# A fused attention and expert block on one core: the query side reads turned rows back from device memory, its steps move one place earlier, and the residual's bias is one operation

## The chip, the cores and the metric

One core of a Trainium2 chip. The metric is device time in microseconds (us), lower is better. Shapes: x is 8 x 2048 rows of 256 floats; everything is float32 (some matmuls take operands split into a high and a low part).

## The reference, cut to what matters

```
q, k, v = heads(x @ Wq + bq), heads(x @ Wk + bk), heads(x @ Wv + bv)      # 16 heads of 16
qp = relu(q @ rw) + 1e-6 ;  kp = relu(k @ rw) + 1e-6                       # 64 features a head
kv = sum over a sequence of kp' v
out = (qp @ kv) / (qp . sum(kp) + 1e-6) ;  x1 = layernorm(x + out @ Wo + bo)
prob = 4 heads' top-8 experts of 1024, from x1 @ Wrq @ keys (exp, products of two halves, keep, normalise)
y = (silu(x1 @ Wg + bg) * (x1 @ Wu + bu)) @ Wd + bd  +  (silu(x1 @ down') * prob) @ up
x2 = layernorm(x1 + y)
```

## The kernel before

The rows are cut into 32 groups of 512; four groups make a sequence. After a start that takes the key side of groups 0 to 3, the program is a loop of **rounds** (`body`, called by `schedule`), numbered from 4 to 38. In round `it` five stages run side by side, each on its own group: the key side ("kv") on group it, the query side of attention ("at") on group m = it - 4, the choice of experts ("rt") on it - 5, the two feed-forward products ("ff") on it - 6, and the last layernorm on it - 7. So rounds 7 to 31 hold all stages. In rounds 8, 12, ..., 32 a finished sequence is folded into attention's weights as well ("fold", "consts").

A round has 8 **slots**, c = 0 to 7, one for each 128 columns of the feed-forward. In a slot PE runs a fixed frame: gate(c), up(c), [choice of experts rt(c/2) where c is even], dots(c), transposes pt(c), and the output matmuls of slot c - 1 in two halves. The frame has three **places**, early, mid and late, where one step of the query side can stand (`AT_EARLY`, `AT_MID`, `AT_LATE`: every third entry of `AT_SEQ`), and likewise places for the key side's steps (`KV_SEQ`). The order in each engine's program is thus written out; an engine runs it strictly in that order.

Steps of the query side: turn0, turn1 (transposes of the group's rows `xb`, 4 matmuls each; ACT copies them to `xbT`, which is `qp[:, 2:4]`), q0, q1 (projection; ACT writes the high parts, DVE the low parts), qp0 to qp7 (features; ACT applies relu), den0 + num0 and den1 + num1 (4 + 4 matmuls with attention's weights), divide0, divide1 (on DVE), wo0, wo1, and at the end of the round next0, next1 (transposes of x1). The key side has turn, k, v, kp0 to kp7 and sum; ACT reads each kp out of PSUM.

All steps but gate, up, dots and the outputs share four PSUM banks, `step_bank`. A **planner** (`take`, line by line through the whole program) gives each use the bank that by its tables `WORK` and `HOLD` comes free first; the table entry for kp is `"kp": 2.0`. At run time PE waits before each use until the reader of the use before it in that bank is done:

```
def free(eng, *use):
    k, nth = place[use]
    if nth:
        eng.wait_ge(bank_read[k], nth)
```

Readers: DVE reads rt(t) in `scores(t)` (L1123), ACT reads kp at L856. In slot 2 and 4 ACT runs, in this order, exp(t) of the scores (`rt_use`, L892, with a table load before and after), then the late kp, then the next slot's silu of gate (L917). In odd slots `mask` (L906, L911) waits for that silu, then POOL's products `spread` (L479) and DVE's `keep` and `add_head` (L1147, L1157, L1160) follow, and then the next slot's scores. In each odd slot DVE's add_head of head 2 runs beside a product of POOL.

POOL adds attention's bias to `xb` (L466, after turn1), and the feed-forward's bias to the residual, which a DMA brings into `prob` columns that pt(0) to pt(3) have freed (L509, slot 5, two operations). SP's queue, in this order: next key rows (L400), output rows (L403), residual (L407), next query rows `xb` and the copy of x1 (L411, L412).

Of the kernel before, what the change touches and what calls it, by code (L numbers as in the profile page):

```python
# [27 lines left out]
P = 128  # L28


def block_kernel(nc, x, Wq, bq, Wk, bk, Wv, bv, Wo, bo, rw, Wg, bg, Wu, bu, Wd, bd,
# [29 lines left out]
              + [("v", 1)] + KV_TILE[2] + KV_TILE[3])  # L61
    AT_SEQ = ([[("turn", 0)], [("turn", 1)], [("q", 0)], [("q", 1)]] + [[("qp", j)] for j in range(4)] + [[]]
              + [[("den", 0), ("num", 0)], [("divide", 0), ("qp", 4)]] + [[("qp", j)] for j in range(5, 8)] + [[]]
              + [[("den", 1), ("num", 1)], [("divide", 1)], [], [("wo", 0)], [("wo", 1)], []])
    KV_USES = len(KV_SEQ)
# [5 lines left out]
    with ExitStack() as ctx:  # L71
# [56 lines left out]
        gate = sb("gate", P, 2, G)  # L128
        wexp = sb("wexp", P, 2, G)
        y_sb = x1  # L130
        x1_kept = nc.dram_tensor("x1_kept", [NG, P, T, D], F32).ap()
# [28 lines left out]

        xa2_loaded = sem("xa2_loaded")
        k2_high = sem("k2_high")

# [133 lines left out]
        class Lane:  # L297


            def __init__(self, x, xT, k_hl, kp, v, xs, loaded, high):  # L300
                self.x, self.xT, self.k_hl, self.kp, self.v, self.xs = x, xT, k_hl, kp, v, xs
                self.loaded, self.high = loaded, high

        xs_total = xs[:, 2]
        LANES = [Lane(xa, xaT, kT_hl, kp, v_sb, xs[:, 0], xa_loaded, k_high),
                 Lane(xb, xbT, qT_hl, kp2, v2_sb, xs[:, 1], xa2_loaded, k2_high)]
        main, second = LANES

# [53 lines left out]
        def _(sp):  # L362
# [33 lines left out]
            def body(it, par, kv, at, rt, ff, last, batch):
                a, m, n, f = it, it - ATTN_LAG, it - FFN_LAG, it - LAST_LAG
                if a + 1 < NG:
                    sp.wait_ge(*full("kv", a, "turn", 1))
                    sp.dma_start(xa[:], x_groups[a + 1]).then_inc(xa_loaded, 16)  # L400
                if last:
                    sp.wait_ge(y_ready, (f + 1) * T)
                    sp.dma_start(out_groups[f], y_sb[:]).then_inc(y_stored, 16)  # L403
                if ff:
                    sp.wait_ge(*full("pt", n, C // 2 - 1))
                    sp.wait_ge(x1_stored, (n + 1) * 16)
                    sp.dma_start(residual(par), x1_kept[n].rearrange("p (i t) d -> p i (t d)", i=2)).then_inc(res_loaded, 16)  # L407
# [11 lines left out]
        def _(pool):  # L419
# [39 lines left out]
            def body(it, par, kv, at, rt, ff, last, batch):  # L459
                a, m, s, n, f = it, it - ATTN_LAG, it - ROUTE_LAG, it - FFN_LAG, it - LAST_LAG  # L460
                if at:
                    pool.wait_ge(xb_loaded, (m + 1) * 16)
                    pool.wait_ge(*full("at", m, "turn", 1))
                    if m == 0:
                        pool.wait_ge(bo_ready, 2)
                    pool.tensor_tensor(xb[:], xb[:], bcast(bo_sb[:].unsqueeze(1), [P, T, D]),  # L466
                                       ALU.add).then_inc(xb_bias, 1)
# [20 lines left out]
                for c in range(C):  # L488
                    t, odd = divmod(c, 2)
                    kv_adds(KV_FIRST[c])  # L490
                    if rt and odd:
                        spread(t, 2)
                    if last and c == 0:
                        norm_scale(y_dve, (f + 1) * Y_STEPS, ln2_pool, f, mv2, rstd2, rstd2_ready)
                    kv_adds(KV_EARLY[c])
                    if rt and odd:
                        spread(t, 3)
                    if at and c == 6:
                        norm_scale(at_dve, (m + 1) * AT_STEPS, ln1_pool, m, mv1, rstd1, rstd1_ready)
                    if rt and not odd:  # L500
                        spread(t, 0)
                    kv_adds(KV_LATE[c])
                    if rt and not odd:
                        spread(t, 1)
                    if ff and c == 5:
                        pool.wait_ge(res_loaded, (n + 1) * 16)
                        rows = residual(par).rearrange("p i (t d) -> p i t d", t=2)
                        for i in range(2):
                            pool.tensor_tensor(rows[:, i], rows[:, i], bcast(bd_sb[:].unsqueeze(1), [P, 2, D]),  # L509
                                               ALU.add).then_inc(res_bias, 1)  # L510

# [4 lines left out]
        def _(pe):  # L516
# [144 lines left out]
            def body(it, par, kv, at, rt, ff, last, batch):  # L661
# [14 lines left out]
                def at_use(kind, j):  # L676
# [3 lines left out]
                    free(pe, "at", m, kind, j)  # L680
                    if kind == "turn":
                        if j == 0:
                            pe.wait_ge(xb_loaded, (m + 1) * 16)
                        mm = turn(at_bank, xb, j)
                    elif kind == "q":
                        pe.wait_ge(*drained("at", m, "turn", 1))
                        mm = project(at_bank, wq_sb, xbT, j)
# [121 lines left out]
        def _(act):  # L809
# [31 lines left out]
            def kv_use(a, kind, j):  # L841
# [5 lines left out]
                if kind == "turn":  # L847
                    if j == 0 and i:
                        before = a - 1 if a > 2 * FILL else a - 2
                        act.wait_ge(xs_added, before + before // BG + 1)  # L850
                    read_by(act.activation(lane.xT[:, j, :], bank[:], ACT.Identity,
                                           accum_out=lane.xs[:, j:j + 1]), "kv", a, kind, j)
# [10 lines left out]
            def body(it, par, kv, at, rt, ff, last, batch):  # L863
# [3 lines left out]
                def at_use(kind, j):  # L867
# [3 lines left out]
                    act.wait_ge(*full("at", m, kind, j))  # L871
                    if kind == "turn":
                        read_by(act.copy(xbT[:, j, :], at_bank[:]), "at", m, kind, j)
                    elif kind == "q":
                        highs(qT_hl, j, at_bank, bq_sb, q_high)
# [84 lines left out]
        def _(dve):  # L960
# [102 lines left out]
            def body(it, par, kv, at, rt, ff, last, batch):  # L1063
# [121 lines left out]
                def y_rows():  # L1185
# [6 lines left out]
                    dve.wait_ge(x1_stored, (min(m, NG)) * 16)  # L1192
                    dve.wait_ge(res_bias, (f + 1) * 2)
                    rows = residual(other).rearrange("p i (t d) -> p i t d", t=2)
# [88 lines left out]
```

## Time and profile before

| | |
|---|---|
| runs shown | 3479.89, 3481.85, 3484.04 us |
| median | 3481.85 us |
| profiled execution, its own time | 3480.97 us |
| its span, first to last instruction | 3479.1 us |
| granted clock of TensorE, mean | 0.989 |

PE is TensorE's matmuls, PEld its weight loads, DVE VectorE, ACT ScalarE, POOL GpSimd, SP SyncE. In a timeline a row reads: start us, busy us, engine, line, operation, written<-read, count, and in brackets the idle time before it with what ended it. Matmuls overlap, so a step's price on PE is best read from the start of one row to the start of the next. Line numbers are those of the kernel before.

### The profile page before, as it was taken

How to read it: one execution, taken by the hardware profiler on the slowest of the kernel's cores; microseconds unless marked ns; L12 is line 12 of the kernel's file. 1: busy time of each engine (PE TensorE's matmuls, PEld its weight loads, DVE VectorE, ACT ScalarE, POOL GpSimd, SP SyncE). 2: the span in 40 equal slices, each digit the busy share in tenths (PEclk: the TensorE clock that was granted, in tenths of full speed). 3: DMA queues.
4: the chain of work that ended last, by engine and by line, in shares of the span. 5: the costliest groups of instructions: out<-in, count | busy, mean ns of one | idle time of the engine just before them, and what ended most of it. 6: DMA issues, size and time to landing. Idle time of an engine off the chain costs nothing.

```text
span 3479.1 us, 48605 instructions
## 1 busy us (share of the span) xinstructions
PE 3362.4 (97%) x17888; PEld 2641.6 (76%) x17888; DVE 2870.6 (83%) x5316; ACT 1991.4 (57%) x2886; POOL 1301.9 (37%) x788
## 2 busy tenths in 40 slices
PE   8779999999999999999999999999999999999988
PEld 6457877777777777877777877777877777777767
DVE  4688878988888888888888887888888888888873
ACT  4456556555556555566556566556556565555541
POOL 0234333334333434343334343344333344434441
PEclk9889999999999999999999999999999999999999
DMA  4000000100001000000001000100000000000000
GB/s 122 25 19 31 19 19 31 31 25 31 19 19 31 31 25 31 19 19 31 31 25 31 19 19 31 31 25 31 19 19 31 31 19 25 25 19 25 13 19 19
DMA packets 36762, 94.35 MB, mean 27 GB/s; under 512 B 6832, under 2 KB 11184, under 8 KB 36528
## 3 DMA queue, kind: packets, MB, share of 16 engines
q1 hardware_dynamic: 36528, 91.25, 8.2%
q8 instruction: 145, 2.38, 0.3%
q14 instruction: 89, 0.73, 0.1%
HBM read 57.68 MB, written 33.55 MB: 26 GB/s over the span
## 4 chain that ended last, share of the span: by engine, by line
PE 82%; DVE 7%; ACT 6%; issue 3%; POOL 2%; DMA 0%; SPq 0%; POOLq 0%; ACTq 0%; DVEq 0%
PE ring L672 26%; PE y_bank L757 11%; PE y_bank L759 11%; PE step_bank L574 6%; PE step_bank L566 5%; PE step_bank L672 4%; PE step_bank L610 3%; PE step_bank L602 3%; PE step_bank L701 3%; PE step_bank L691 3%; PE step_bank L745 3%; DVE prob L1160 2%; PE step_bank L560 2%; POOL grid L479 1%; ACT prob L911 1%
## 5 line engine op out<-in xcount | busy, mean ns | idle before, releaser
L479 POOL TENSOR_TENSOR grid<-ex 128x1024 f32<-128x1024 f32 x512 | 994.5, 1950 | 1469.6 <-ACT ex L892 726.5
L757 PE MATMUL y_bank<-wd_sb,gate 128*128 128x256 f32 x2048 | 622.8, 386 | 9.2 <-DVE wexp L1182 9.2
L759 PE MATMUL y_bank<-up_sb,wexp 128*128 128x256 f32 x2048 | 613.3, 381 | 0.0
L1160 DVE SCALAR_TENSOR_TENSOR prob<-grid,narrow,prob 128x1024 f32<-128x1024 f32 x256 | 580.2, 2266 | 9.0
L672 PE MATMUL ring<-x1T_hl,downT_hl 128*128 128x512 f32 x1536 | 421.2, 410 | 23.8 <-ACT gate L917 23.7
L672 PE MATMUL ring<-x1T_hl,wg_hl 128*128 128x512 f32 x1536 | 430.1, 415 | 5.0 <-DVE gate L1176 5.0
L759 PEld LDWEIGHTS y_bank<-up_sb,wexp 128*128 128x128 f32 x2048 | 391.8, 191 | 54.2
L1147 DVE SCALAR_TENSOR_TENSOR grid<-grid,best 128x1024 f32<-128x1024 f32 x256 | 343.6, 1342 | 107.0 <-POOL grid L479 105.1
L672 PE MATMUL ring<-x1T_hl,wu_hl 128*128 128x512 f32 x1536 | 421.2, 409 | 0.0
L757 PEld LDWEIGHTS y_bank<-wd_sb,gate 128*128 128x128 f32 x2048 | 362.0, 192 | 70.8 <-issue 37.9
L672 PEld LDWEIGHTS ring<-x1T_hl,wu_hl 128*128 128x128 f32 x1536 | 281.9, 188 | 119.6 <-issue 42.9
L672 PEld LDWEIGHTS ring<-x1T_hl,downT_hl 128*128 128x128 f32 x1536 | 277.4, 189 | 97.3 <-ACT gate L917 36.8
L672 PEld LDWEIGHTS ring<-x1T_hl,wg_hl 128*128 128x128 f32 x1536 | 286.1, 189 | 75.8 <-issue 14.9
L856 ACT ACTIVATE kp<-step_bank 128x512 f32<-128x512 f32 x233 | 137.3, 590 | 339.4 <-PE step_bank L602 339.3
L1176 DVE SCALAR_TENSOR_TENSOR gate<-ring,bu_sb,gate 128x512 f32<-128x512 f32 x256 | 190.5, 744 | 165.6 <-PE ring L672 157.9
L892 ACT ACT_TABLE_LOAD x124 | 159.1, 1283 | 284.0 <-DVE ex L1125 283.4
L922 ACT ACTIVATE wexp<-ring 128x512 f32<-128x512 f32 x256 | 152.3, 595 | 283.0 <-PE ring L672 282.2
L917 ACT ACTIVATE gate<-ring,bg_sb 128x512 f32<-128x512 f32 x256 | 176.3, 689 | 237.8 <-PE ring L672 235.4
L906 ACT ACTIVATE grid<-grid,narrow 128x1024 f32<-128x1024 f32 x256 | 294.1, 1149 | 11.4 <-POOL grid L479 6.8
L1086 DVE RECIPROCAL x<-x 128x512 f32<-128x512 f32 x64 | 213.9, 3343 | 2.6 <-ACT x L884 2.6
L672 PE MATMUL step_bank<-route_hl,x1T_hl 128*128 128x512 f32 x768 | 198.6, 394 | 1.8 <-DVE x1T_hl L970 1.8
L466 POOL TENSOR_TENSOR xb<-xb,bo_sb 128x1024 f32<-128x1024 f32 x32 | 75.5, 2358 | 303.7 <-PE step_bank L560 303.7
(168 smaller groups left out, 5551.2 us busy)
## 6 DMA issues: line engine op xcount, KB each, us to landing
xb<-in_L_attn_x SPq DMA_DIRECT2D x34, 512.0 KB, 4.2
x_kept<-x SPq DMA_DIRECT2D x32, 512.0 KB, 5.1
prob<-x_kept SPq DMA_DIRECT2D x32, 512.0 KB, 3.6
out_y<-x SPq DMA_DIRECT2D x32, 512.0 KB, 2.7
xa<-in_L_attn_x SPq DMA_DIRECT2D x30, 512.0 KB, 3.5
prob<-in_L_ffn_down_embed SPq DMA_DIRECT2D x1, 1024.0 KB, 6.2
prob<-in_L_ffn_Wg SPq DMA_DIRECT2D x1, 1024.0 KB, 10.0
prob<-in_L_ffn_Wu SPq DMA_DIRECT2D x1, 1024.0 KB, 10.7
```

What stands on the lines that cost most here:

```text
L479: pool.tensor_tensor(grid[:, h % 2], bcast(ex[:, h, 0:NX].unsqueeze(2), [P, NX, NK]), bcast(ex[:, RH + h, 0:NK].unsqueeze(1), [P, NX, NK]) ...
L566: mm = pe.matmul(bank[:], w[:, k, e * P:(e + 1) * P], srcT[:, k, :], start=(k == 0), stop=(k == KD - 1))
L574: mm = pe.matmul(bank[:, (t - t0) * D:(t - t0 + 1) * D], srcT[:, k, t * P:(t + 1) * P], w[:, k, :], start=(k == 0), stop=(k == KD - 1))
L672: mm = pe.matmul(bank[:], st if swap else wt, wt if swap else st, start=(k == 0 and i == 0), stop=(k == KD - 1 and i == 2))
L757: pe.matmul(rows, gate[:, c % 2, t * P:(t + 1) * P], wd_sb[:, c, :], start=(c == 0 and t % 2 == 0), stop=False, skip_group_check=True)
L759: mm = pe.matmul(rows, wexp[:, c % 2, t * P:(t + 1) * P], up_sb[:, c, :], start=False, stop=(c == C - 1), skip_group_check=True)
L906: act.activation(g, g, ACT.Prelu, bias=drop[:, h:h + 1], alpha=STEEP).then_inc(bent, 1)
L917: act.activation(gate[:, c % 2], ring[c % 2][:], ACT.Silu, bias=bg_sb[:, c:c + 1]).then_inc(ring_act, 1)
L1086: at_steps.mark(dve.reciprocal(rows, rows))
L1147: marks["keep", h] = rt_steps.mark(dve.scalar_tensor_tensor(out=g, in0=g, scalar=best[:, h, TOP - 1:TOP], in1=g, op0=ALU.is_ge, op1=ALU.mult))
L1160: ins = dve.scalar_tensor_tensor(out=row, in0=g, scalar=rz[:, h:h + 1], in1=row, op0=ALU.mult, op1=ALU.add, accum_out=mass[:, 0:1] if h == ...
L1176: dve.scalar_tensor_tensor(out=gate[:, c % 2], in0=ring[1 - c % 2][:], scalar=bu_sb[:, c:c + 1], in1=gate[:, c % 2], op0=ALU.add, op1=ALU. ...
```

## The change

Three edits. (1) After a group's key side has turned its rows (`xT`), SP stores them to device memory (`xT_kept`, one DMA of 512 KB a group); in the round before their query side they are loaded into `xbT` once num1 has been issued and read its operands. turn0 and turn1 of the query side, their ACT copies, and PE's wait for `xb` are gone; POOL's bias on `xb` no longer waits for turn1. (2) `AT_SEQ` loses its two turn entries and gets one empty entry ahead and one behind: q1 stands late in slot 0 instead of early in slot 1, qp to wo1 one place earlier, den0 and num0 late in slot 2 instead of early in slot 3, den1 and num1 late in slot 4 instead of early in slot 5. divide0 and divide1 on DVE now stand ahead of slot 3's and slot 5's product with up(c). The planner runs anew over the new order, with its tables as they were. (3) The residual's bias is one POOL operation in slot 4, ahead of the first product of that slot, instead of two at the end of slot 5.

```diff
-    AT_SEQ = ([[("turn", 0)], [("turn", 1)], [("q", 0)], [("q", 1)]] + [[("qp", j)] for j in range(4)] + [[]]
+    AT_SEQ = ([[], [("q", 0)], [("q", 1)]] + [[("qp", j)] for j in range(4)] + [[]]
               + [[("den", 0), ("num", 0)], [("divide", 0), ("qp", 4)]] + [[("qp", j)] for j in range(5, 8)] + [[]]
-              + [[("den", 1), ("num", 1)], [("divide", 1)], [], [("wo", 0)], [("wo", 1)], []])
+              + [[("den", 1), ("num", 1)], [("divide", 1)], [], [("wo", 0)], [("wo", 1)], [], []])
...
+        xT_kept = nc.dram_tensor("xT_kept", [NG, P, KD, G], F32).ap()
...
+            def keep_turned(a):
+                sp.wait_ge(*drained("kv", a, "turn", 0))
+                sp.wait_ge(*drained("kv", a, "turn", 1))
+                sp.dma_start(xT_kept[a], in_lane(a)[0].xT[:]).then_inc(in_lane(a)[0].kept, 16)
...
                     sp.dma_start(xa[:], x_groups[a + 1]).then_inc(xa_loaded, 16)
+                if kv:
+                    keep_turned(a)
...
+                if at and m + 1 < NG:
+                    lane, i = in_lane(m + 1)
+                    sp.wait_ge(*full("at", m, "num", 1))
+                    sp.wait_ge(lane.kept, (i + 1) * 16)
+                    sp.dma_start(xbT, xT_kept[m + 1]).then_inc(xbT_loaded, 16)
                 if at:
                     sp.wait_ge(x1_ready, (m + 1) * T)
...
                     pool.wait_ge(xb_loaded, (m + 1) * 16)
-                    pool.wait_ge(*full("at", m, "turn", 1))
...
+                    if ff and c == C // 2:
+                        pool.wait_ge(res_loaded, (n + 1) * 16)
+                        rows = residual(par).rearrange("p i (t d) -> p i t d", t=2)
+                        pool.tensor_tensor(rows, rows, bcast(bd_sb[:].unsqueeze(1).unsqueeze(1), [P, 2, 2, D]),
+                                           ALU.add).then_inc(res_bias, 1)
                     if rt and not odd:
                         spread(t, 0)
...
-                    if ff and c == 5:
-                        pool.wait_ge(res_loaded, (n + 1) * 16)
-                        rows = residual(par).rearrange("p i (t d) -> p i t d", t=2)
-                        for i in range(2):
-                            pool.tensor_tensor(rows[:, i], rows[:, i], bcast(bd_sb[:].unsqueeze(1), [P, 2, D]),
-                                               ALU.add).then_inc(res_bias, 1)
...
-                    if kind == "turn":
-                        if j == 0:
-                            pe.wait_ge(xb_loaded, (m + 1) * 16)
-                        mm = turn(at_bank, xb, j)
-                    elif kind == "q":
-                        pe.wait_ge(*drained("at", m, "turn", 1))
+                    if kind == "q":
+                        pe.wait_ge(xbT_loaded, (m + 1) * 16)
                         mm = project(at_bank, wq_sb, xbT, j)
...
+                        act.wait_ge(lane.kept, i * 16)
...
-                    if kind == "turn":
-                        read_by(act.copy(xbT[:, j, :], at_bank[:]), "at", m, kind, j)
...
-                    dve.wait_ge(res_bias, (f + 1) * 2)
+                    dve.wait_ge(res_bias, f + 1)
```

**PE, slot 0, from rt(0) to gate(1) of round 15, before** (route_hl is rt(0), ident_r,xa the key side's turn, ident_r,xb the query side's, downT_hl dots(0), ident_r,prob pt(0), qp,wq_sb the projection q; bank_readN counts the readers of step_bank N):

```order
L672 MATMUL step_bank<-route_hl,x1T_hl 128x512 [waits bank_read2,bank_read1,bank_read3]
L672 MATMUL ring<-x1T_hl,downT_hl 128x512 [waits ring_act]
L560 MATMUL step_bank<-ident_r,xb 128x128 [waits bank_read1]
L745 MATMUL step_bank<-ident_r,prob 128x128 [waits bank_read0,prob_ready]
L560 MATMUL step_bank<-ident_r,xa 128x128 [waits bank_read3]
L566 MATMUL step_bank<-qp,wq_sb 128x512 [waits bank_read1]
L672 MATMUL ring<-x1T_hl,wg_hl 128x512 [waits h_ready]
L566 MATMUL step_bank<-qp,wq_sb 128x512 [waits bank_read1,bank_read3]
```

**The same place after:**

```order
L692 MATMUL step_bank<-route_hl,x1T_hl 128x512 [waits bank_read0,bank_read3,bank_read2]
L692 MATMUL ring<-x1T_hl,downT_hl 128x512 [waits ring_act]
L586 MATMUL step_bank<-qp,wq_sb 128x512 [waits xbT_loaded,bank_read2]
L761 MATMUL step_bank<-ident_r,prob 128x128 [waits bank_read3,prob_ready]
L580 MATMUL step_bank<-ident_r,xa 128x128 [waits bank_read1]
L586 MATMUL step_bank<-qp,wq_sb 128x512 [waits xbT_loaded,bank_read0]
L692 MATMUL ring<-x1T_hl,wg_hl 128x512 [waits h_ready]
```

q1 stands ahead of gate(1), and the planner has given it bank 0, which in this round rt(0) filled: q1 waits for the read of rt(0). Before, q1 had the bank of the key side's turn1. So it is in rounds 7 to 31 but for those with a fold, where q1 has q0's bank.

**PE, end of slot 2 and start of slot 3, before** (rw_hl,kT_hl is kp, L701 with four waits den0, with one wait num0; the outputs between are left out):

```order
L745 MATMUL step_bank<-ident_r,prob 128x128 [waits bank_read3]
L602 MATMUL step_bank<-rw_hl,kT_hl 128x256 [waits bank_read3,bank_read1]
L672 MATMUL ring<-x1T_hl,wg_hl 128x512 [waits h_ready]
L701 MATMUL step_bank<-qp,kv_blocks 32x512 [waits bank_read1,bank_read3,blocks_ready,bank_read0]
L701 MATMUL step_bank<-qp,kv_blocks 32x512 [waits bank_read2]
L672 MATMUL ring<-x1T_hl,wu_hl 128x512 [waits ring_act]
```

**The same place after:**

```order
L761 MATMUL step_bank<-ident_r,prob 128x128 [waits bank_read0]
L622 MATMUL step_bank<-rw_hl,kT_hl 128x256 [waits bank_read2]
L717 MATMUL step_bank<-qp,kv_blocks 32x512 [waits bank_read2,bank_read3,blocks_ready,bank_read0]
L717 MATMUL step_bank<-qp,kv_blocks 32x512 [waits bank_read2]
L692 MATMUL ring<-x1T_hl,wg_hl 128x512 [waits h_ready]
```

den0 and num0 stand ahead of gate(3), and num0 has the bank that kp0 filled just before it, in all of rounds 6 to 31; before, num0 had the bank of rt(1). In the same way num1 has the bank of kp3: there it had it before too, but num1 now stands ahead of gate(5).

**ACT, slot 2 into slot 3, after** (ex is exp(1), kp the read of kp0, x<-step_bank the read of den0, gate the silu of gate(3)):

```order
L907 ACT_TABLE_LOAD [waits rt_dve]
L907 ACTIVATE ex<-ex 128x576 [waits bank_read1]
L873 ACTIVATE kp<-step_bank 128x512 [waits bank_full3]
L899 ACTIVATE x<-step_bank,consts 128x512 [waits x1_stored,bank_read3,y_stored,bank_full2]
L932 ACT_TABLE_LOAD [waits y_full]
L932 ACTIVATE gate<-ring,bg_sb 128x512 [waits ring_full]
```

The read of kp0 still stands behind exp(1), which waits for DVE's scores(1); the read of den0 has come in ahead of the silu of gate(3).

## Rows read from the trace of the kernel before

**Rows 1.** The page: busy time, share of the span and instructions of each engine.
```profile
PE 3362.4 (97%) x17888; PEld 2641.6 (76%) x17888; DVE 2870.6 (83%) x5316; ACT 1991.4 (57%) x2886; POOL 1301.9 (37%) x788
```

**Rows 2.** Stretches: us, busy by engine, clock, DMA share, GB/s; rounds 15, 16, 33.
```profile
1159.58:1262.38 102.80, 102.80 (x547) 80.94 (x545) 89.24 (x165) 62.19 (x90) 40.90 (x25) 1.00 0.09 26
1262.38:1370.60 108.22, 106.45 (x599) 83.66 (x597) 89.23 (x172) 62.42 (x90) 40.62 (x24) 1.00 0.07 25
3027.30:3122.90 95.60, 89.09 (x419) 69.91 (x417) 82.55 (x155) 53.28 (x74) 40.76 (x23) 0.98 0.07 23
```

**Rows 3.** Timeline of PE, round 15, slots 0 and 1.
```profile
1166.16 0.60 PE L560 MATMUL step_bank<-ident_r,xb 128*128 128x128 f32 x4
1166.60 0.60 PE L745 MATMUL step_bank<-ident_r,prob 128*128 128x128 f32 x4
...
1167.58 1.95 PE L566 MATMUL step_bank<-qp,wq_sb 128*128 128x512 f32 x4
1168.97 1.95 PE L672 MATMUL ring<-x1T_hl,wg_hl 128*128 128x512 f32 x6
```

**Rows 4.** Timeline of PE, round 15: gate(3), den0 with num0, gate(5).
```profile
1195.84 1.73 PE L672 MATMUL ring<-x1T_hl,wg_hl 128*128 128x512 f32 x6
1197.50 1.92 PE L701 MATMUL step_bank<-qp,kv_blocks 128*32 128x512 f32 x16
...
1219.79 1.72 PE L672 MATMUL ring<-x1T_hl,wg_hl 128*128 128x512 f32 x6
```

**Rows 5.** Timeline of DVE, round 15: scores(0), scores(1), keep and add beside POOL's bias.
```profile
1169.23 0.69 DVE L1123 TENSOR_TENSOR ex<-step_bank,top 128x512 f32<-128x512 f32 x1
...
1195.49 0.69 DVE L1123 TENSOR_TENSOR ex<-step_bank,top 128x512 f32<-128x512 f32 x1
...
1214.28 1.28 DVE L1160 SCALAR_TENSOR_TENSOR prob<-grid,narrow,prob 128x1024 f32<-128x1024 f32 x1
...
1237.26 1.71 DVE L1147 SCALAR_TENSOR_TENSOR grid<-grid,best 128x1024 f32<-128x1024 f32 x1
1239.01 2.20 DVE L1160 SCALAR_TENSOR_TENSOR prob<-grid,narrow,prob 128x1024 f32<-128x1024 f32 x1
```

**Rows 6.** Timeline of ACT, round 15: q0's highs, silu(1), mask(0), exp(1), kp0, silu(3), kp3.
```profile
1169.57 1.39 ACT L838 ACTIVATE qT_hl<-step_bank,bq_sb 64x512 fp32r<-64x512 f32 x2 [1.21 <-PE step_bank L566]
...
1174.28 0.69 ACT L917 ACTIVATE gate<-ring,bg_sb 128x512 f32<-128x512 f32 x1
...
1176.72 0.48 ACT L901 ACTIVATE narrow<-best,narrow 128x1 f32<-128x1 f32 x2 [0.23 <-DVE narrow L1141]
1177.23 1.15 ACT L906 ACTIVATE grid<-grid,narrow 128x1024 f32<-128x1024 f32 x1
...
1196.39 1.28 ACT L892 ACT_TABLE_LOAD   x1 [3.91 <-DVE ex L1125]
...
1198.27 0.58 ACT L856 ACTIVATE kp<-step_bank 128x512 f32<-128x512 f32 x1
...
1200.17 0.69 ACT L917 ACTIVATE gate<-ring,bg_sb 128x512 f32<-128x512 f32 x1
...
1220.50 0.58 ACT L856 ACTIVATE kp<-step_bank 128x512 f32<-128x512 f32 x1
```

**Rows 7.** Timeline of POOL, round 15: attention's bias, the residual's bias.
```profile
1166.91 2.37 POOL L466 TENSOR_TENSOR xb<-xb,bo_sb 128x1024 f32<-128x1024 f32 x1 [8.44 <-PE step_bank L560]
...
1235.62 4.51 POOL L509 TENSOR_TENSOR prob<-prob,bd_sb 128x512 f32<-128x512 f32 x2
```

**Rows 8.** The page, DMA issues: count, KB each, us from issue to landing.
```profile
x_kept<-x SPq DMA_DIRECT2D x32, 512.0 KB, 5.1
```

**Rows 9.** Waits of PE in its timeline (rounds 16, 33).
```profile
1287.75 1.98 PE L566 MATMUL step_bank<-xaT,wk_sb 128*128 128x512 f32 x4 [1.71 <-ACT qp L877]
...
3117.86 1.02 PE L757 MATMUL y_bank<-wd_sb,gate 128*128 128x256 f32 x2 [2.30 <-DVE wexp L1182]
```

**Rows 10.** Stretch behind the second of those waits, columns as in rows 2.
```profile
3117.86:3121.23 3.37, 3.37 (x8) 2.66 (x9) 3.33 (x2) 0.00 (x0) 1.90 (x1) 0.53 0.30 118
```

More of the change, by code:

```diff
@@ L161, in block_kernel @@
         xa2_loaded = sem("xa2_loaded")
+        xaT_kept, xbT_kept, xbT_loaded = sem("xaT_kept"), sem("xbT_kept"), sem("xbT_loaded")
         k2_high = sem("k2_high")
@@ L297, in block_kernel, with __init__ @@
         class Lane:
-            def __init__(self, x, xT, k_hl, kp, v, xs, loaded, high):
+            def __init__(self, x, xT, k_hl, kp, v, xs, loaded, kept, high):
                 self.x, self.xT, self.k_hl, self.kp, self.v, self.xs = x, xT, k_hl, kp, v, xs
-                self.loaded, self.high = loaded, high
+                self.loaded, self.kept, self.high = loaded, kept, high
         xs_total = xs[:, 2]
-        LANES = [Lane(xa, xaT, kT_hl, kp, v_sb, xs[:, 0], xa_loaded, k_high),
-                 Lane(xb, xbT, qT_hl, kp2, v2_sb, xs[:, 1], xa2_loaded, k2_high)]
+        LANES = [Lane(xa, xaT, kT_hl, kp, v_sb, xs[:, 0], xa_loaded, xaT_kept, k_high),
+                 Lane(xb, xbT, qT_hl, kp2, v2_sb, xs[:, 1], xa2_loaded, xbT_kept, k2_high)]
         main, second = LANES
@@ L389, in _ @@
                     sp.dma_start(lane.x[:], x_groups[2 * r + k]).then_inc(lane.loaded, 16)
+                for k in range(2):
+                    keep_turned(2 * (r - 1) + k)
             sp.wait_ge(*full("kv", 2 * FILL - 2, "turn", 1))
@@ L394, in _ @@
             sp.dma_start(xb[:], x_groups[0]).then_inc(xb_loaded, 16)
+            for k in range(2):
+                keep_turned(2 * FILL - 2 + k)
+            sp.wait_ge(*full("kv", 2 * FILL - 1, "v", 1))
+            sp.wait_ge(xbT_kept, FILL * 16)
+            sp.wait_ge(xaT_kept, 16)
+            sp.dma_start(xbT, xT_kept[0]).then_inc(xbT_loaded, 16)
             def body(it, par, kv, at, rt, ff, last, batch):
@@ L871, in at_use @@
                     act.wait_ge(*full("at", m, kind, j))
-                    if kind == "turn":
-                        read_by(act.copy(xbT[:, j, :], at_bank[:]), "at", m, kind, j)
-                    elif kind == "q":
+                    if kind == "q":
                         highs(qT_hl, j, at_bank, bq_sb, q_high)
```

## Prediction

> **What bounds the kernel now.** First the page's busy times: PE is busy in 97% of the span, DVE in 83%, POOL in 37% [rows 1]. That is an average, so next the stretches by round, from gate(0) to gate(0). In round 15 PE is busy in all of 102.80 us: it never waits, and its order is a sum of work. The fold's round 16 takes 108.22 with 1.8 of waits; in the tail's round 33 PE is busy for 89.09 of 95.60, so there others set the pace [rows 2]. Rounds 7 to 31 are of the first two kinds, 19 without and 6 with a fold. There a matmul taken from PE is time gained, but only as long as PE still finds at each place what it waits for. So I read PE's rows for the places of the change, and then when the reader of each step bank is done.
>
> **What PE loses in work.** From a turn's start to that of the next step are 0.44 us [rows 3], two turns 0.87. Over 25 rounds that is 22 us. ACT's two copies go too; ACT is busy for 62 of 102.80 us [rows 2], and they count only where ACT's order is on the path (below).
>
> **What moves: three waits.** All times are in round 15's frame, gate(0) at 1159.58.
>
> *q1.* It now precedes gate(1), at PE's 1168.97 - 0.87 = 1168.10 [rows 3], in the bank of rt(0). DVE reads that last in scores(0), until 1169.23 + 0.69 = 1169.92 [rows 5]. So PE, which had no wait, stands for 1.8. POOL's bias on `xb` (2.37, [rows 7]) no longer waits for turn1, and falls beside DVE's keep and add of the end of the round before. The nearest row of such company is keep beside POOL's other bias, 1.71 against 1.28 [rows 5]. I add that 0.4 (bounds 0 and 0.9, what add loses there): q1 starts at 1170.3, a wait of 2.2. On ACT, q1's high parts now precede exp(0). High parts start 2.0 after their matmul (1169.57 against 1167.58, [rows 3, 6]), so at 1172.3, 2.7 later than those of q0 that stood there. exp(0), silu(1) and mask(0) follow. From silu(1) to mask(0) were 2.95, in which q1's high parts (1.39) go and a qp's read comes (priced as kp's, 0.58), and 0.23 was idle [rows 6]. So mask(0) is later by 2.7 - 1.39 + 0.58 - 0.23 = 1.65, and I take the chain behind it (POOL's product, DVE's keep, add and scores(1), ACT's exp(1)) as late by as much. Bounds: 0, if slack swallows it, and 2.7.
>
> *num0.* It now precedes gate(3), right behind kp0 and in kp0's bank. ACT's read of kp0 stands behind exp(1), whose table load waited 3.91 us for DVE's scores(1); it ended at 1198.27 + 0.58 = 1198.85 [rows 5, 6]. den0 with num0 take 1197.50 to 1199.35, the 1.85 between two neighbours, num0 half of it. PE alone would come to num0 at 1195.84 - 0.87 + 0.92 = 1195.9 [rows 3, 4], 2.95 ahead of the read even if nothing else moved. With the 1.65 the read ends at 1200.5: PE has lost 4.6 by then, q1's wait within it. Gate(3) follows at 1201.4, where the same work stood at 1195.84 + 1.85 = 1197.69: **+3.75** a round, the turns' gain included.
>
> *num1.* It now precedes gate(5), in kp3's bank. PE comes to it 23.95 - 0.92 = 23.0 after gate(3) [rows 4], at 1224.4. The read of kp3 ended at 1220.50 + 0.58 = 1221.08, behind exp(2), which hangs on slot 3's chain from silu(3). That began at 1200.17 [rows 6]; now it follows gate(3) (its matmuls take 1.66, [rows 4]) and begins about 1203.0: 2.8 later. Then the residual's bias: one operation at the end of slot 3's products, where it meets keep and add of head 3. In slot 5 those took 1.71 and 2.20 instead of 1.28 each, 1.35 in all [rows 5]; I take that (bounds: 0 if they don't meet, 1.9 if the add of head 2 meets it as well). The read then ends at 1221.08 + 4.15 = 1225.2, 0.8 behind PE: **+0.8** (0 to 1.4). DVE's time in slot 5 gets shorter by the same 1.35, but PE doesn't wait there.
>
> **Other rounds.** The sum of a round is 4.55. In fold rounds the fold's matmuls stand ahead of q1, which takes q0's bank, so part of the wait is covered; between -0.87 and +4.55 I take +1, that is +6 in all. Round 6 has num0 in kp0's bank too, but fewer stages: +2. The tail's four rounds have no kp and shed the turns and DVE's collisions: -1 each.
>
> **What I cost at nothing.** The store of turned rows and their load are 512 KB each, with 5.1 us to land [rows 8]; the DMA engines are busy for 0.09 of a round [rows 2]. The store goes out at about 1169, ahead of the output's store on SP, which waits longer for its rows. The load goes out once num1 has read its operands, over 40 us ahead of the next q0. If it were late, q0 would wait by as much. It stands ahead of x1's copy on SP, and is gone long before. divide0 and divide1 move ahead of the product with up(c) on DVE; that product's reader is a slot away. One bias operation in place of two: between 2.37, POOL's row of the same size, and 4.51 [rows 7]; POOL is busy for 40.90 of 102.80, and the next product waits for exp(2).
>
> **Sum.** 19 x 4.55 + 6 + 2 - 4 = +90.5 us on the profiled execution's 3480.97: 3571.5. The median of the runs is 0.9 above that execution, so I forecast **3572 us**.
>
> On the collisions: the trace has POOL's bias of 4.51 cost DVE 1.35, under a third of it [rows 5, 7]. The Trainium skill (SBUF — State Buffer, "SBUF: two separate sides") calls the port pair that VectorE and GpSimd share an exclusive lock: whoever starts first keeps it for its whole instruction, and the other fully blocks. By that, keep, starting some 0.6 into a bias of 2.37, would lose about 1.75 instead of 1.35, an estimate that adds 0.4 x 19 = 8 us. The sum goes by the row.
>
> **Rivals.** (1) *Only PE's work goes.* If kp0's read comes 2.95 or more earlier against gate(0), no bank wait holds. The point that decides is DVE's scores(1). For it: DVE idles for 13.5 us of the round [rows 2], so its order could close up. Against it: mask(0) now hangs on q1's high parts, later and not earlier. Gain 25 x 0.87 = 22: 3460, **faster**. Chance 0.11. (2) *Gain and wait cancel*, or the new places are neutral because kp0's read comes about 2 us sooner: 3482. Chance 0.05. (3) *Only num0 waits*; q1 delays nothing behind it, num1 finds its bank: 2.95 - 0.87 = 2.1 a round, 19 x 2.1 - 4 = +36, **3517**. For it: slack that a chain swallows is easily overlooked. Against: the 0.23 of idle on ACT is little [rows 6]. Chance 0.18. (4) *The forecast*: 0.54. (5) *The clock falls as well.* After a wait of 2.30 in round 33 TensorE ran at a granted 0.53 (its 1.2 GHz level) for 3.37 us, at a cost of 3.37 x 0.47 = 1.6; after one of 1.71 it stayed at 2.4 GHz [rows 9, 10]. The new waits, 2.2 and 2.4, are of that size. After q1 the loss would be hidden in num0's wait; after num0 it counts: 19 x 1.6 = 30, **3602**. Chance 0.12. The Trainium skill (TensorE: Matmul & The Clock Gate, "What's actually happening") has the throttled clock as the default that activity releases, which speaks for (5); the row of 1.71 shows that not every pause brings it back.
>
> **How the numbers follow.** My own case with its bounds reaches from 3540 (chain late by less) to 3600 (2.7 late). Down to 3510 the range takes in rival 3, up to 3612 rival 5 with a little more; outside are rivals 1 and 2 and small rests. A measurement of this kernel tells about 0.2%, 7 us, from no change. Faster is rival 1, 0.11; same is rival 2, 0.05; slower is all the rest, 0.84.
>
> **What would show it.** In the profile after: PE busy for less than a round; rounds such as 15 at about 107 us; waits of PE ahead of q1 of about 2 with DVE's scores as releaser, ahead of num0 of about 2.4 on ACT's read of kp, ahead of num1 under 1.4; the turns on `xb` gone; POOL's residual bias as one row of 2.4 to 4.5, with keep and add of slot 3 longer and those of slot 5 at 1.28; mask(0) about 19.3 us behind gate(0) instead of 17.65. I am wrong if rounds take about 102, if kp0's read ends within 36.3 us of gate(0), or if q0 waits for its load.

## The result, and the profile after

The changed kernel takes **3588.42 us** (median of 4 runs, 3586.83 to 3593.29), beside 3480.87 for the kernel before on the same chip: a ratio of 1.0312, 95% interval 1.0298 to 1.0327. That is slower by 107.5 us; 3572 were forecast, with 3510 to 3612 as the range.

The page after, busy times and the chain that ended last, against [rows 1]:

```profile
PE 3373.8 (94%) x17632; PEld 2617.2 (73%) x17632; DVE 2851.4 (79%) x5316; ACT 1956.9 (55%) x2822; POOL 1312.5 (37%) x756
...
PE 35%; DVE 28%; ACT 19%; issue 13%; POOL 4%; SPq 0%; ACTq 0%; DVEq 0%; DMA 0%; POOLq 0%
```

PE has 256 matmuls fewer, the turns, and is busy for 11 us more than before (3362.4). Where the time came from is read by rounds. These are sums of rounds of the profiled execution (3589.75 us), each from gate(0) to gate(0) in the timeline of PE, in us, with the change in the last column:

| stretch | before | after | change | forecast |
|---|---|---|---|---|
| ahead of round 6 | 219.9 | 219.6 | -0.3 | 0 |
| round 6 | 104.8 | 107.4 | +2.6 | +2 |
| 19 rounds without a fold, of 7 to 31 | 1953.4 | 2043.9 | +90.5 | +86.5 |
| their median round | 102.79 | 107.23 | +4.44 | +4.55 |
| 6 rounds with a fold | 650.9 | 663.5 | +12.6 | +6 |
| rounds 32 to 36 | 472.0 | 475.2 | +3.2 | -4 |

Stretches after (rounds 14, 15, 16 and 34; columns as in [rows 2]):

```profile
1085.03:1192.26 107.23, 102.66 (x538) 79.79 (x537) 88.04 (x165) 61.11 (x88) 41.06 (x24) 1.00 0.10 35
1192.26:1300.89 108.63, 104.30 (x539) 80.46 (x537) 88.23 (x165) 61.11 (x88) 41.31 (x25) 0.98 0.10 35
1300.89:1411.58 110.69, 107.73 (x590) 83.20 (x589) 89.75 (x172) 61.22 (x88) 41.02 (x24) 0.98 0.10 34
3228.32:3324.61 96.29, 88.91 (x410) 68.75 (x409) 83.15 (x155) 52.30 (x72) 40.34 (x23) 0.98 0.08 28
```

Round 14 is the typical one: PE is busy for 102.66, where round 15 before had 102.80 without a gap, and idle for 4.57. Its idle time stands in PE's timeline: q0 and pt(0) (no wait), then q1, gate(1), dots(1), den0, num0, gate(3), num1.

```profile
1091.15 1.88 PE L586 MATMUL step_bank<-qp,wq_sb 128*128 128x512 f32 x4
1092.87 0.60 PE L761 MATMUL step_bank<-ident_r,prob 128*128 128x128 f32 x4
...
1095.80 1.98 PE L586 MATMUL step_bank<-qp,wq_sb 128*128 128x512 f32 x4 [1.90 <-DVE ex L1138]
1097.22 1.94 PE L692 MATMUL ring<-x1T_hl,wg_hl 128*128 128x512 f32 x6
...
1103.27 1.65 PE L692 MATMUL ring<-x1T_hl,downT_hl 128*128 128x512 f32 x6 [0.56 <-ACT gate L932]
...
1123.79 1.06 PE L717 MATMUL step_bank<-qp,kv_blocks 128*32 128x512 f32 x8 [0.28 <-DVE v_sb L1031]
1125.72 1.07 PE L717 MATMUL step_bank<-qp,kv_blocks 128*32 128x512 f32 x8 [0.87 <-ACT kp L873]
1126.72 1.66 PE L692 MATMUL ring<-x1T_hl,wg_hl 128*128 128x512 f32 x6
...
1150.83 1.07 PE L717 MATMUL step_bank<-qp,kv_blocks 128*32 128x512 f32 x8 [0.96 <-ACT kp L873]
```

The three bank waits are there, each with the releaser that was named: DVE's scores (L1138), ACT's read of kp (L873) twice. ACT in that round, mask(0), kp0, silu(3), kp3:

```profile
1104.19 1.15 ACT L921 ACTIVATE grid<-grid,narrow 128x1024 f32<-128x1024 f32 x1
...
1125.09 0.58 ACT L873 ACTIVATE kp<-step_bank 128x512 f32<-128x512 f32 x1
...
1128.42 0.69 ACT L932 ACTIVATE gate<-ring,bg_sb 128x512 f32<-128x512 f32 x1 [0.86 <-PE ring L692]
...
1150.20 0.58 ACT L873 ACTIVATE kp<-step_bank 128x512 f32<-128x512 f32 x1
```

mask(0) starts 1104.19 - 1085.03 = 19.16 after gate(0); it was 17.65, and 19.3 was forecast. DVE in the same round (keep at its start; in slot 3 the add of head 2, then keep and add of head 3), then POOL (bias on `xb`, last product of slot 3, the residual's bias):

```profile
1086.71 1.65 DVE L1162 SCALAR_TENSOR_TENSOR grid<-grid,best 128x1024 f32<-128x1024 f32 x1
...
1137.58 3.03 DVE L1175 SCALAR_TENSOR_TENSOR prob<-grid,narrow,prob 128x1024 f32<-128x1024 f32 x1
...
1141.13 2.81 DVE L1162 SCALAR_TENSOR_TENSOR grid<-grid,best 128x1024 f32<-128x1024 f32 x1
1143.97 1.28 DVE L1175 SCALAR_TENSOR_TENSOR prob<-grid,narrow,prob 128x1024 f32<-128x1024 f32 x1
```

```profile
1083.87 3.41 POOL L487 TENSOR_TENSOR xb<-xb,bo_sb 128x1024 f32<-128x1024 f32 x1
...
1137.62 1.91 POOL L500 TENSOR_TENSOR grid<-ex 128x1024 f32<-128x1024 f32 x1 [3.13 <-DVE prob L1172]
1139.49 3.37 POOL L524 TENSOR_TENSOR prob<-prob,bd_sb 128x1024 f32<-128x1024 f32 x1
```

Both biases now meet a keep, which takes 1.65 and 2.81, where a DVE operation of this size takes 1.28 alone [rows 5], and POOL's own operation takes 3.4 instead of the 2.37 of [rows 7]: it begins while DVE's add is still running.

### The profile page after: what moved, and what is told of

It is laid out like the page before. It is cut to its first block, busy times and chain, and to the rows that moved or that the text cites. A ratio compares the mean times of both kernels' runs of the same rounds, so it can differ in the third digit from the quotient of the medians.

```text
span 3587.9 us, 48061 instructions
## 1 busy us (share of the span) xinstructions
PE 3373.8 (94%) x17632; PEld 2617.2 (73%) x17632; DVE 2851.4 (79%) x5316; ACT 1956.9 (55%) x2822; POOL 1312.5 (37%) x756
## 4 chain that ended last, share of the span: by engine, by line
PE 35%; DVE 28%; ACT 19%; issue 13%; POOL 4%; SPq 0%; ACTq 0%; DVEq 0%; DMA 0%; POOLq 0%
PE ring L692 10%; DVE prob L1175 7%; DVE grid L1162 5%; PE step_bank L594 5%; POOL grid L500 4%; PE y_bank L773 4%; ACT grid L921 4%; PE y_bank L775 4%; ACT prob L926 3%; DVE prob L1172 3%; PE step_bank L586 3%; DVE top L1135 3%; ACT L932 2%; PE step_bank L630 2%; PE step_bank L717 2%
## 5 line engine op out<-in xcount | busy, mean ns | idle before, releaser
L500 POOL TENSOR_TENSOR grid<-ex 128x1024 f32<-128x1024 f32 x512 | 1011.2, 1982 | 1540.3 <-ACT ex L907 794.7
L1162 DVE SCALAR_TENSOR_TENSOR grid<-grid,best 128x1024 f32<-128x1024 f32 x256 | 391.0, 1527 | 284.9 <-POOL grid L500 283.1
L1175 DVE SCALAR_TENSOR_TENSOR prob<-grid,narrow,prob 128x1024 f32<-128x1024 f32 x256 | 551.5, 2154 | 7.9
L692 PE MATMUL ring<-x1T_hl,wu_hl 128*128 128x512 f32 x1536 | 399.7, 396 | 0.0
L873 ACT ACTIVATE kp<-step_bank 128x512 f32<-128x512 f32 x233 | 136.9, 589 | 416.1 <-PE step_bank L622 416.0
L692 PEld LDWEIGHTS ring<-x1T_hl,wu_hl 128*128 128x128 f32 x1536 | 289.9, 189 | 64.0
L477 POOL TENSOR_SCALAR rstd<-mv 128x4 f32<-128x4 f32 x64 | 15.2, 237 | 602.7 <-DVE mv L1091 602.7
```

The source lines that it names most:

```text
L500: pool.tensor_tensor(grid[:, h % 2], bcast(ex[:, h, 0:NX].unsqueeze(2), [P, NX, NK]), bcast(ex[:, RH + h, 0:NK].unsqueeze(1), [P, NX, NK]) ...
L692: mm = pe.matmul(bank[:], st if swap else wt, wt if swap else st, start=(k == 0 and i == 0), stop=(k == KD - 1 and i == 2))
L1162: marks["keep", h] = rt_steps.mark(dve.scalar_tensor_tensor(out=g, in0=g, scalar=best[:, h, TOP - 1:TOP], in1=g, op0=ALU.is_ge, op1=ALU.mult))
L1175: ins = dve.scalar_tensor_tensor(out=row, in0=g, scalar=rz[:, h:h + 1], in1=row, op0=ALU.mult, op1=ALU.add, accum_out=mass[:, 0:1] if h == ...
```

## The experiments

Each ran against the kernel before on the same chip; before's median was 3479 to 3483 us in all of them. Behind each time stand its ratio to that and the 95% interval of the ratio. "Steady" is the median round without a fold in the profiled execution.

**Places back, the rest as changed.**

```diff
-    AT_SEQ = ([[], [("q", 0)], [("q", 1)]] + ...
+    AT_SEQ = ([[], [], [("q", 0)], [("q", 1)]] + ...
```

> Turned rows from device memory and the one bias as in the changed kernel, but the query side's steps at the places of the kernel before (the two turn entries left empty). Bank theory (the loss is PE waiting at the new places for banks that DVE and ACT still hold): no wait is left, PE saves the turns, 25 x 0.87 less some dearer neighbours: 3455 to 3470 us, rounds of 102.0 to 102.4. Rival, the bias theory (the residual's bias beside slot 3's keep and add makes the chain late): slower than before, 3490 to 3520.

Measured: 3494.65 us, 1.0036 (1.0023 to 1.0048), steady 103.49. So 94 of the 107 us hang on the new places; but the turns' time isn't gained, and 12 us are lost: at the old places the time is in the bias theory's range. Waits of PE's weight loads in one round (total, times, longest, in us), and POOL and DVE in slot 3 (view by view):

```profile
PEld step_bank L717 <- ACT kp L873: 1.1, 1, 1.1
...
PEld ring L692 <- DVE gate L1191: 0.9, 1, 0.9
```

```profile
1106.42 3.38 POOL L524 TENSOR_TENSOR prob<-prob,bd_sb 128x1024 f32<-128x1024 f32 x1
```

```profile
1108.07 2.81 DVE L1162 SCALAR_TENSOR_TENSOR grid<-grid,best 128x1024 f32<-128x1024 f32 x1
```

With the turns gone PE comes to gate(1) sooner, and its weight load waits for DVE's product with up(0); PE's own rows show a gap of only 0.10 there (q0 from 1061.30 to 1063.18, gate(1) at 1063.28), although q0's start and gate(1)'s lie 1.98 apart instead of 1.39 [rows 3]: the rows of two steps overlap, and a wait takes that overlap first. And keep loses 1.53; in slot 5 num1's weight load then waits 1.1 for ACT's read of kp.

**Other banks for num0 and num1; for q1; for all three** (one number each in the planner's table; both are shown, as the third run has them).

```diff
-        ... "kp": 2.0, ... "rt": 8.0
+        ... "kp": 6.0, ... "rt": 12.0
```

> The changed kernel, but the planner's table holds a kp's bank for 6 instead of 2: num0 then has the bank of rt(1), num1 that of pt(4), q1 still that of rt(0). Bank theory: the waits of 0.87 ahead of num0 and 0.96 ahead of num1 go in 25 rounds (the second alone in fold rounds): 3588 - 19 x 1.83 - 6 x 0.96 = 3548; rounds of 105.4. Rival, the chain theory (ACT and DVE are themselves late, because q1's high parts stand ahead of exp(0)): PE stops a little later for a silu or for weights instead, 3575 to 3590.

Measured: 3542.87 us, 1.0171 (1.0157 to 1.0185). num0's and num1's waits are gone, q1's stays at 1.89, as the bank theory had it; the 6 steady rounds with a granted clock of 1.00 take 104.94, the other 13, at 0.98, about 106.4. The planner may move other uses as well, but PE's other waits in such a round are those of the changed kernel (dots(1) 0.5, den0 0.3).

> The changed kernel, but the planner's table holds rt's bank for 12 instead of 8: q1 then has the bank of the key side's turn1, num0 and num1 still those of kp0 and kp3. Bank theory: q1's wait of 1.89 goes, and with it the late silu(1) ahead of dots(1) (0.56) and some of ACT's lateness, but PE then comes to num0 sooner than kp0's read, and waits there for about 2.2 instead of 0.87: a gain of 1.0 to 1.5 a round, 3560 to 3570. Chain theory: the whole chain comes 1.9 sooner with q1, num0's wait stays near 0.9: 3588 - 19 x 2.4 = 3542.

Measured: 3584.92 us, 1.0294 (1.0280 to 1.0308), which neither theory had. q1 and num0 in PE's timeline:

```profile
1096.79 1.98 PE L586 MATMUL step_bank<-qp,wq_sb 128*128 128x512 f32 x4 [1.44 <-ACT xaT L868]
...
1126.71 1.07 PE L717 MATMUL step_bank<-qp,kv_blocks 128*32 128x512 f32 x8 [0.87 <-ACT kp L873]
```

q1 stands behind rt(0), pt(0) and turn1 in PE's order, and the bank of turn1 is still being copied by ACT: 1.44 instead of 1.89. num0's wait stays at 0.87, so the chain theory holds in this one point: kp0's read moves with gate(1), and what q1 loses isn't given back at num0. So the steady round is shorter by 0.47 (106.76 for 107.23), 13 us in sum; some 10 of them are lost again ahead of round 7, in the fold's rounds and in the tail.

> The changed kernel with both table entries raised (kp 6, rt 12): q1 has the bank of turn1, num0 that of pt(2), num1 that of pt(4), at the changed kernel's places. Bank theory: nearly all waits go, rounds come to PE's own 102.7 plus den0's 0.3: about 3490, no slower than 3500. Chain theory: DVE and ACT can't feed a round of 103 with q1's parts ahead of exp(0) and the residual's bias in slot 4; PE waits at dots or at the outputs, 3530 to 3570.

Measured: 3532.26 us, 1.0141 (1.0125 to 1.0156), steady 104.56, of which 2.3 are waits: q1 1.45, dots(1) 0.56, den0 0.31. The two holds together bring 56 us, and the time is in the chain theory's range. The rest of the loss stays, on other readers: q1 waits for ACT's copy of turn1, dots(1) for ACT's silu, den0 for DVE's read of v. Whether some other order of banks would leave no wait at these places was not tried.

**The old residual bias** (two operations at the end of slot 5), first with the old places, then with the new ones.

```diff
-                    if ff and c == C // 2:
...
+                    if ff and c == 5:
...
+                        for i in range(2):
```

> Turned rows from device memory alone: the query side's steps at the places of the kernel before, the residual's bias as before (two operations at the end of slot 5). Collision theory (the places-only run lost 12 us because POOL's bias in slot 4 holds up DVE's keep by 1.53 a round, and POOL's bias on xb another keep by 0.38): the first is gone, the second stays; rounds of 102.2 to 102.6, 3465 to 3475. Rival, traffic or order (PE's other steps get dearer when the turns go, whatever POOL does): rounds of 103.5 again, 3490 to 3497.

Measured: 3481.49 us, 1.0001 (0.9992 to 1.0009), steady 103.03. This is the turned rows alone: no gain, though two turns a round are gone; between the two theories. By stretches, the 19 steady rounds are longer by 4.8 us in sum, and the stretch ahead of round 6 is shorter by 5.2 (214.7 for 219.9). num1's weight load no longer waits for ACT's read of kp.

> The changed kernel with its new places, but the residual's bias as before (two operations at the end of slot 5). Collision theory: keep in slot 3 back at 1.28, exp(2) 1.5 sooner, num1's wait of 0.96 goes in 25 rounds: 3588 - 24 = 3564; q1's and num0's waits stay. Rival (the bias is off the path, kp3's read is late for another reason): 3585 to 3590.

Measured: 3555.27 us, 1.0207 (1.0193 to 1.0221). num1's wait is gone and steady rounds at the full clock take 106.02, 1.2 less than 107.23. So the bias in slot 4 costs 33 us at the new places and 13 at the old ones (3494.65 against 3481.49).

**POOL's bias on `xb` held back**, with the new places.

```diff
                     pool.wait_ge(xb_loaded, (m + 1) * 16)
+                    pool.wait_ge(*full("at", m, "q", 0))
```

> The changed kernel, but POOL's bias on xb waits until q0 has been computed, about as late as turn1 let it start before. Collision theory: keep at the start of a round back from 1.65 to 1.27, q1's wait from 1.89 to 1.5, and all behind it 0.38 sooner in 19 rounds: 3580. Rival (slack takes it up): 3586 to 3590.

Measured: 3570.29 us, 1.0252 (1.0237 to 1.0268). q1's wait is 1.52 instead of 1.89, steady rounds 106.83: 0.4 x 19 = 8 us as expected. Of the other 10, 6 come from the clock (a granted 0.98 in 6 of these 19 rounds of the changed kernel, 1.00 in all 19 here) and 5 from the fold's rounds.

**Both biases held back, old places.**

```diff
+                    pool.wait_ge(*full("at", m, "q", 0))
...
+                        if rt:
+                            wait(pool, rt_dve, s * RT_STEPS + (t - 1) * len(RT_TILE) + RT_AT[("add", 3)])
```

> The candidate for a version that beats both: turned rows from device memory, the old places, the one bias in slot 4, but each of POOL's two bias operations waits until DVE has passed the operations that it met: the residual's until the add of head 3 in slot 3, that on xb until q0. Collision theory: DVE's keep at 1.28 everywhere, PE saves the turns: rounds of 101.9 to 102.2, 3481 - 25 x 0.7 = 3463, between 3458 and 3468. Rival (DVE's and ACT's chain can't run a round below 102.8 whatever POOL does): 3478 to 3485.

Measured: 3538.84 us, 1.0164 (1.0150 to 1.0178): far off, the wrong way, and the most telling run. DVE, two of the smallest operations of a round, and POOL beside the second:

```profile
1075.29 1.23 DVE L1143 TENSOR_TENSOR ex<-top 128x64 f32<-128x64 f32 x1
...
1122.26 2.29 DVE L1189 TENSOR_TENSOR prob<-prob,narrow 128x1 f32<-128x1 f32 x1
```

```profile
1122.19 2.35 POOL L527 TENSOR_TENSOR prob<-prob,bd_sb 128x1024 f32<-128x1024 f32 x1 [4.35 <-DVE prob L1178]
```

An operation on one element a partition, 0.16 elsewhere, took 2.29: it ended with POOL's, which had started 0.07 before it. It did so in 31 places of this run, and never in the kernels before and after.

**The biases in DVE's gaps, old places**: the residual's behind slot 3's last step on `prob`, after which DVE reads PSUM for some 2.6 us; that on `xb` behind pt(0).

```diff
+                    if ff:
+                        pool.wait_ge(*full("pt", n, 0))
...
+                        if rt:
+                            pool.wait_ge(prob_ready, s * T + t)
```

> Turned rows, the old places, one bias in slot 4, but POOL's bias operations are put where DVE for some 2.6 us has no operation on two tensors of SBUF: the residual's after the last of slot 3's mass steps (prob_ready), that on xb after pt(0). Lock theory (POOL's operation and DVE's operations on two SBUF tensors exclude each other whole, so that in the run with guards a 128x1 operation took 2.29 instead of 0.16): no DVE operation of slots 0, 1, 3, 4 and 5 is longer than alone, rounds of 102.0 to 102.4, 3460 to 3472. Rival (without collisions too PE can't run ahead: gate(1) waits for DVE's product with up(0)): rounds of 102.7 to 102.9, 3476 to 3485.

Measured: **3464.14 us, 0.9956 (0.9943 to 0.9970)**, faster than both kernels, if only by 0.4% than the one before. The residual's bias, and a stretch of one round:

```profile
1105.85 2.36 POOL L528 TENSOR_TENSOR prob<-prob,bd_sb 128x1024 f32<-128x1024 f32 x1 [4.73 <-DVE prob L1190]
```

```profile
1049.34:1151.99 102.65, 102.46 (x539) 79.83 (x537) 87.88 (x165) 61.33 (x88) 38.25 (x23) 1.00 0.12 37
```

The time came out as expected, but not from where it was expected: steady rounds are 102.65, hardly under 102.79. The gain is in rounds 32 to 36 (460.3 against 472.0) and ahead of round 6 (213.5 against 219.9).

> The same two waits of POOL, and the holds of 6 and 12, with the changed kernel's new places. Lock theory with bank theory: of the run with both holds (rounds of 104.5) q1's wait of 1.45 for ACT's read of turn1, dots(1)'s 0.56 and den0's 0.31 stay, since none hangs on POOL: 3525 to 3533. Rival (the holds only moved the loss, DVE's lateness is what is left): rounds below 103.7, 3505 to 3515.

Measured: 3536.15 us, 1.0163 (1.0149 to 1.0177): slower than either theory had it. In this order POOL's bias, held until pt(0), still meets a small operation of DVE (0.77, and 0.21 in the run with both holds); DVE comes to the four scales of the last layernorm a little later, and a product of POOL gets in ahead of the last of them:

```profile
1084.85 0.77 DVE L1144 TENSOR_TENSOR ex<-top 128x64 f32<-128x64 f32 x1
...
1089.46 2.99 DVE L1223 TENSOR_SCALAR x<-x,mv,rstd 128x256 f32<-128x256 f32 x4
```

```profile
1083.18 2.35 POOL L489 TENSOR_TENSOR xb<-xb,bo_sb 128x1024 f32<-128x1024 f32 x1 [9.71 <-PE step_bank L765]
...
1090.40 1.90 POOL L502 TENSOR_TENSOR grid<-ex 128x1024 f32<-128x1024 f32 x1 [3.55 <-ACT ex L911]
```

The product starts 0.03 before the last scale, which takes 2.01 instead of 0.41; with both holds the four scales took 1.38. The copy of v that den0 waits for then ends 1.15 later after gate(0) than with both holds, and den0 waits 1.46 instead of 0.31.

**Where the gain came from**: the kernel before with the one bias in that gap; and the gap kernel with DVE's product with up(0) ahead of the layernorm's sums (this edit is shown).

```diff
+                    if ff and c == 0:
+                        ff_h(c)
                     if last and c == 0:
                         y_rows()
...
-                    if ff:
+                    if ff and c:
                         ff_h(c)
```

> The kernel before (turns on PE, its own places) with one edit: the residual's bias as one operation in slot 4, after the last of slot 3's mass steps. If the gain of the run with POOL's operations in DVE's gaps came from the bias alone: the tail's five rounds lose some 11 us as there, the steady rounds stay at PE's 102.8, the head at 220: 3468 to 3472. If it came from the turned rows: 3478 to 3484.

Measured: 3471.10 us, 0.9972 (0.9962 to 0.9982), rounds 32 to 36 461.5: the bias alone gives 10 us, in the tail, where DVE sets the pace. Its stretch ahead of round 6 is not shorter (222.5), while the five runs with turned rows at the old places have 213.5 to 217.1 there; so the other part of the gap kernel's gain goes with the turned rows.

> The run with POOL's operations in DVE's gaps, and on DVE the product with up(0) ahead of the last layernorm's sums in slot 0, so that gate(1) finds its weight load free: the 0.56 us that gate(1)'s weight load waited for DVE go. If that wait is what keeps the steady rounds at 102.65 although the turns' 0.87 are gone: rounds of 102.0 to 102.2, 3448 to 3455. Rival (the wait passes on to the next step that DVE or ACT feeds, q1's high parts or the silu): rounds above 102.5, 3460 to 3465.

Measured: 3459.28 us, 0.9939 (0.9927 to 0.9952), steady 102.53. gate(1)'s weight load no longer waits, and yet rounds are no shorter than 102.5: in time neither theory, in rounds the rival. Against the run before (0.9956) the intervals overlap, so the two aren't told apart.

## Why the prediction was right, and which terms were off

**The mechanism** was right, and so were its moments. *q1* was to start 10.7 after gate(0) and started at 10.77. The collision ahead of it was to cost 0.4 and cost 0.38. mask(0) came at 19.16 for 19.3; kp0's read ended 1125.67 - 1085.03 = 40.6 after gate(0) for 40.9. num1's wait was 0.96 for 0.8. The wait ahead of num0 was 0.87, though, where about 2.4 stood among the signs: dots(1) and den0 waited 0.56 and 0.28 before it, which nobody had priced. That left the round as forecast, because num0 starts when kp0's read is done, and the read came at the forecast time. The holds show that these waits are the cause and not only beside it: given other banks, num0's and num1's went, and 45 us with them. For q1 the evidence is smaller: no run of these took its wait away, but where it was shorter by 0.37 and by 0.45 the round was shorter by 0.40 and by 0.47.

**The turns' 0.87** seems to be missing: PE's busy time in a steady round fell by only 0.14 (102.80 to 102.66), and the waits ahead of num0 sum to 1.90 + 0.56 + 0.28 + 0.87 = 3.6 for 4.6. The two differences belong together, and the sum hit, +4.44 for +4.55. Rows of neighbouring steps overlap; a wait ends the overlap, and that part counts as busy. The key side's k ahead of dots(1) takes 1.88 without the gap, for 1.32 before, and dots(1) 1.48 for 1.79: 0.25 more for the two. Round 15 before, then round 14 after, up(1), the key side's k, dots(1) and the next step:

```profile
1172.08 1.96 PE L672 MATMUL ring<-x1T_hl,wu_hl 128*128 128x512 f32 x6
1173.87 1.88 PE L566 MATMUL step_bank<-xaT,wk_sb 128*128 128x512 f32 x4
1175.19 1.95 PE L672 MATMUL ring<-x1T_hl,downT_hl 128*128 128x512 f32 x6
1176.98 0.62 PE L691 MATMUL step_bank<-qT_hl,rw_hl 128*128 128x512 f32 x2
```

```profile
1099.46 1.52 PE L692 MATMUL ring<-x1T_hl,wu_hl 128*128 128x512 f32 x6
1100.83 1.88 PE L586 MATMUL step_bank<-xaT,wk_sb 128*128 128x512 f32 x4
1103.27 1.65 PE L692 MATMUL ring<-x1T_hl,downT_hl 128*128 128x512 f32 x6 [0.56 <-ACT gate L932]
1104.75 0.62 PE L707 MATMUL step_bank<-qT_hl,rw_hl 128*128 128x512 f32 x2
```

den0 takes 1.06 to the next start, without the gap, for 0.92. q0 is not dearer in sum: it takes 1.72 ahead of pt(0) and took 1.39 ahead of gate(1) [rows 3], but up(1), which no longer follows a q, takes 1.37 for 1.79.

At the old places the turns' time is gained first and lost again later. In the last run pt(0) starts 6.13 after gate(0) instead of 7.02 [rows 3], but the median round is only 0.26 shorter. Waits of its weight loads in one round:

```profile
PEld step_bank L711 <- ACT qp L896: 0.5, 1, 0.5
PEld step_bank L626 <- DVE kv_sum L1044: 0.4, 1, 0.4
...
PEld step_bank L711 <- DVE kT_hl L1015: 0.3, 1, 0.3
```

The first stands ahead of gate(2): gate(1) still starts 1.07 sooner than before (8.32 after gate(0) for 9.39), but there a qp waits for ACT's read of an earlier one and starts only 0.67 sooner (22.61 for 23.28). The rest goes in steps of about 0.1, two of them behind the other two waits; for the others no row names a releaser, and that stays open.

**Three terms were mis-sized.** The profiled execution lies 18 us above the 3571.5 that was worked out for it: 4 in the steady rounds (the clock's 6.5 less 2 from their median), 6.6 in the fold's rounds, 7.2 in the tail, and little in round 6.

- *"In fold rounds ... I take +1"*: +2.1 was measured. num1's wait of 0.96 stands there too and dots(1)'s 0.56; with the old bias the fold's rounds sum to 655.1, with kp held longer to 654.3, for 663.5.
- *The tail, "-1 each"*: +3.2 over its five rounds. The bias's collision isn't shed there, it only moves to slot 3; with it gone, rounds 32 to 36 shrink by 11 us. The prediction had looked for no gain or loss of DVE in the one stretch where DVE sets the pace.
- *Rival 5, the clock*, priced at nothing in the forecast, came true in part. The 19 steady rounds lie 2043.9 - 19 x 107.23 = 6.5 us over their median, nearly all of it in 6 rounds with a granted 0.98. One of them, after q1's wait; the granted clock stands ahead of the DMA share:

```profile
1203.03 3.41 PE L586 MATMUL step_bank<-qp,wq_sb 128*128 128x512 f32 x4 [1.89 <-DVE ex L1138]
1205.45 2.62 PE L692 MATMUL ring<-x1T_hl,wg_hl 128*128 128x512 f32 x6
```

```profile
1202.46:1205.86 3.40, 2.83 (x5) 1.29 (x5) 2.83 (x5) 0.07 (x1) 0.00 (x0) 0.64 0.76 299
```

The same stretch of round 14:

```profile
1095.23:1098.63 3.40, 2.83 (x9) 1.71 (x10) 2.92 (x6) 0.85 (x3) 0.00 (x0) 1.00 0.77 299
```

The same wait of 1.9, beside the same DMA load, left the clock at 2.4 GHz in round 14 and brought it to a mean of 0.64 in round 15. It was not hidden behind num0's wait, as the rival had it: kp0's read moves with gate(1), and the round was longer by 1.4.

**Rivals 1 to 3** fall: each needed slack in DVE's and ACT's chain, and kp0's read came 1.4 later against gate(0) (40.6 for 39.3 [rows 6]).

**On the collisions** the prediction took 1.35 from a row against an exclusive lock. keep lost 1.53, the add after it nothing, and POOL 1.0 besides. The Trainium skill (SBUF — State Buffer, "SBUF: two separate sides") was nearer in kind: the runs with 2.29 for a 128x1 operation, and with 3.4 for POOL's 2.36 beside DVE's add, agree with an exclusive lock for the whole instruction. The row of 4.51 had misled: its two operations run from 1235.62 to 1237.89 and from 1237.85 to 1240.13, and keep, from 1237.26 to 1238.97, ended between their ends.

## What to carry to other kernels

A step that is moved ahead in PE's order meets its buffer's last reader sooner: look up who reads the bank it gets, and when, before counting what the move saves, and give a planner the hold times of the new order. Place an operation of POOL on SBUF by an event, where DVE works out of PSUM; a gap in POOL's own time says nothing, and even an operation of DVE on one element can pay for the whole of POOL's. A gain that is taken from one stage's bound (PE in the steady rounds) and one from another's (DVE in the tail) are to be measured apart.

## What the runs showed of the hardware that was not expected

- One 128x1 operation of DVE on SBUF took 2.29 us beside POOL's 2.35, and 0.16 alone; a 128x256 scale that came 0.03 after a POOL product took 2.01, and 0.41 alone; a POOL operation of 2.36 took 3.4 when it met a DVE operation that had begun.
- Equal waits don't bring equal clocks: with q1's wait of about 1.9 the mean granted clock was 0.98 in 6 of 19 steady rounds of the changed kernel, in 10 of 19 of the run with the old bias and in 13 of 19 of the run with kp held longer; in the run with POOL's bias on `xb` held back, where it was 1.52 in most rounds, the clock was 1.00 in all 19.
- The gap in PE's own rows shows only a part of a wait: gate(1)'s 0.9 in the weight loads' waits left a gap of 0.10 and put 0.59 between the starts of two steps.
